# Splitting the running maximum in three bf16 parts, and the router's weights as one stationary matrix

## What is computed

```
log_D = where(tril, cs[:, :, None] - cs[:, None, :], -inf) + ig[:, None, :]
max_log_D = max(log_D, axis=-1)
D_mat = exp(log_D - max_log_D)
C = (q @ k.T) / sqrt(64) * D_mat
h = (C / (maximum(abs(C.sum(-1)), exp(-max_log_D)) + 1e-6)) @ v
x = x + tanh(g_xattn) * layernorm(h) * ln_scale

x2 = layernorm(x)
scores = softmax(x2 @ router_w.T)
topk_w, topk_idx = top_k(scores, 2)
x = x + tanh(g_ffn) * (routed experts(x2) + shared expert(x2))
```

## Time and profile before

| | us |
|---|---|
| median of 3 runs | 1300.96 (1299.69 to 1302.8) |
| the profiled execution | 1299.23 |
| its span in the trace | 1297.7 |

### The profile page before, as it was taken

One profiled execution on the slowest core, in us unless ns is written; L12 is line 12 of the kernel. 1 busy time (PEld: TensorE's weight loads), 2 busy tenths in 40 slices (PEclk: granted clock), 3 DMA queues, 4 the chain that ended last, 5 costly groups with the idle time before them and its releaser, 6 DMA issues.

```text
span 1297.7 us, 23994 instructions
## 1 busy us (share of the span) xinstructions
PE 1111.2 (86%) x6643; PEld 912.9 (70%) x6644; DVE 749.3 (58%) x1940; ACT 387.6 (30%) x852; POOL 478.2 (37%) x368
## 2 busy tenths in 40 slices
PE   3099999999999999999999876999999999999000
PEld 2066888888888888888888764788888888887000
DVE  2835667676677677676667634544444444444365
ACT  1132344443343344343343101233232322322000
POOL 3700021222213220322122335366656657700675
PEclk9565899999999999999999978999999999999555
DMA  6010010111001110111000244555564645331798
GB/s 206 17 48 33 1 64 4 66 65 65 32 32 65 65 59 6 65 48 49 12 23 34 82 168 143 192 173 183 162 194 162 203 153 178 129 113 65 217 301 265
DMA packets 57849, 134.37 MB, mean 104 GB/s; under 512 B 7088, under 2 KB 7088, under 8 KB 57808
## 3 DMA queue, kind: packets, MB, share of 16 engines
q0 software_dynamic: 17472, 59.78, 14.1%
q1 hardware_dynamic: 26128, 48.51, 11.4%
q10 hardware_dynamic: 14208, 25.57, 5.5%
HBM read 83.23 MB, written 50.59 MB: 103 GB/s over the span
## 4 chain that ended last, share of the span: by engine, by line
PE 84%; DVE 6%; DMA 6%; issue 2%; ACT 1%; POOL 1%; DVEq 0%; POOLq 0%; ACTq 0%
PE bank L1141 18%; PE bank L1006 15%; PE bank L1159 9%; PE bank L1017 7%; PE bank L953 6%; PE bank L921 5%; PE bank L944 4%; DMA area<-routed_y,y_at 4%; PE bank L887 4%; PE bank L955 3%; PE bank L1129 3%; PE bank L992 2%; PE bank L966 2%; PE bank L968 2%; PE bank L965 2%
## 5 line engine op out<-in xcount | busy, mean ns | idle before, releaser
L1141 PE MATMUL bank<-w_ring,x2nT 128*128 x960 | 243.7, 403 | 7.1 <-DVE x2nT L1624 7.0
L1006 PE MATMUL bank<-x2nT,w_ring 128*128 128x256 f32 x1536 | 206.3, 293 | 3.2 <-DVE sh_act L1426 3.2
L1141 PEld LDWEIGHTS bank<-w_ring,x2nT 128*128 128x128 f32 x960 | 175.7, 190 | 46.8 <-issue 11.8
L1006 PEld LDWEIGHTS bank<-x2nT,w_ring 128*128 128x128 f32 x1536 | 195.6, 199 | 3.8 <-issue 3.6
L492 POOL DMA_INDIRECT routed_x<-x2n,slot_u x64 | 63.2, 988 | 250.8 <-DVE slot_u L1418 236.2
L1159 PE MATMUL bank<-w_ring,sh_actT 128*128 x480 | 125.4, 396 | 2.3 <-DVE sh_actT L1619 2.3
L513 POOL TENSOR_TENSOR sh_actT<-sh_act,sh_actT 128x256 fp32r<-128x256 f32 x64 | 46.8, 732 | 203.8 <-ACT sh_actT L732 203.8
L609 POOL TENSOR_TENSOR w_ring<-area,one 128x3072 fp32r<-128x3072 f32 x14 | 74.2, 5303 | 114.5 <-PE bank L1159 114.5
L1606 DVE SCALAR_TENSOR_TENSOR ctxT<-ctxT,bank 128x256 f32<-128x256 f32 x80 | 33.7, 421 | 142.5 <-ACT ctxT L834 142.5
L1159 PEld LDWEIGHTS bank<-w_ring,sh_actT 128*128 128x128 f32 x480 | 90.0, 188 | 24.3 <-issue 3.0
L1017 PE MATMUL bank<-w_ring,sh_actT 128*128 128x512 f32 x384 | 102.4, 418 | 2.3 <-DVE sh_act L1426 1.4
(11 more groups left out here) (192 smaller groups left out, 2007.7 us busy)
## 6 DMA issues: line engine op xcount, KB each, us to landing
x2n<-routed_x SPq DMA_DIRECT2D x80, 256.0 KB, 2.7
routed_y<-cs_in ACTq DMA_DIRECT2D x80, 256.0 KB, 2.1
base_out<-in_x_dram SPq DMA_DIRECT2D x16, 512.0 KB, 4.8
cs_in<-in_ctx_dram SPq DMA_DIRECT2D x16, 512.0 KB, 3.5
area<-n_L_ffn_expert_gate_dram POOLq DMA_DIRECT2D x16, 512.0 KB, 4.1
area<-in_L_ffn_expert_up_dram POOLq DMA_DIRECT2D x16, 512.0 KB, 5.8
area<-n_L_ffn_expert_down_dram POOLq DMA_DIRECT2D x16, 512.0 KB, 7.1
out_dram<-area SPq DMA_DIRECT2D x32, 256.0 KB, 4.3
```

Of the source, the lines that this page charges most:

```text
L1006: last = mm(GU[m][:, at:at + S], w[:, w_part, c, m * P:(m + 1) * P], x2nT[:, x_part, c, :], start=(c + p == 0), stop=(c == DC - 1 and p == 2))
L1141: last = mm(bank[2 + t.par][:, :], xtT[:, x_part, t.par, c * P:(c + 1) * P], w_gu[:, bass.ds(slot, 1), w_part, c, :].rearrange("p a i -> p ...
```

## The change

The running maximum is kept in three bf16 parts instead of two fp32r ones, in rows 0, 32 and 64 on; `head_sel` is bf16 as well, and `spread` multiplies 96 rows, which makes its tile 128 x 128, like the mask product's. DVE has two more operations in `rows_end`, and `spread` waits for the eighth of them. The router has `router_wT`, padded with zeros to 128 columns, as stationary matrix and streams 256 tokens past it: 8 products. Their result has the tokens along the columns, so ACT copies 32 rows of it (`logit_row`), and PE turns them back with two float32 products against `pair_ident` (two stacked identities, which also add both parts; 32 rows, a tile of 32 x 128), in the new `logits_pe`, which stands ahead of `shared(G, 1)` on PE. DVE copies the logits from there. The start gets a memset of `router_wT` and the making of `pair_ident` on DVE, and a third selection for `head_sel` on POOL.

```diff
-        head_sel = sb("head_sel", [P, NH, P], F32R)
+        head_sel = sb("head_sel", [P, NH, P], BF16)
-        router_wT = sb("router_wT", [P, DC, 2 * E], F32R)
+        router_wT = sb("router_wT", [P, DC, P], F32R)
+        pair_ident = sb("pair_ident", [2 * E, E])
-        max_parts = sb("max_parts", [FG + NH, 2, S], F32R)
+        max_rest = sb("max_rest", [FG + NH, S])[FG:, :]
+        max_parts = sb("max_parts", [P, 2, S], BF16)
+        logit_row = sb("logit_row", [2 * E, S])
-        row_step = event("row_step", 6)
+        row_step = event("row_step", 8)
...
-                for part in range(2):
+                for part in range(3):
                     select(head_sel[:], 1.0, ALU.not_equal, -FG * part, 1, [[-1, NH], [0, P]])
...
+            def router(b):
+                act.wait_ge(router_made.sem, router_made.upto(b.n))
+                s.copy(logit_row[:, :], SM[0:2 * E, 0:S]).then_inc(logit_row_made.sem, 1)
...
                 if front:
                     max_hi(F)
                 if route:
+                    router(G)
                     shared(G, 0)
...
-                    mm(MB[k][:, at:at + n], head_sel[0:FG + NH, h, :], max_parts[:, b.par, S - n:S],
+                    mm(MB[k][:, at:at + n], head_sel[0:3 * FG, h, :], max_parts[0:3 * FG, b.par, S - n:S],
...
+                for c in range(DC):
+                    for part in range(2):
+                        last = mm(SM[:, 0:S], router_wT[:, c, :], x2nT[:, part, c, :],
+                                  start=(c + part == 0), stop=(c == DC - 1 and part == 1))
+                last.then_inc(router_made.sem, 1)
+
+            def logits_pe(b):
+                pe.wait_ge(wT_copied.sem, 9)
+                pe.wait_ge(logit_row_made.sem, logit_row_made.upto(b.n))
+                apart(pe)
                 for j in range(ST):
-                    for c in range(DC):
-                        for part in range(2):
-                            last = mm(SM[:, j * 2 * E:(j + 1) * 2 * E], x2nT[:, part, c, j * P:(j + 1) * P],
-                                      router_wT[:, c, :], start=(c + part == 0), stop=(c == DC - 1 and part == 1))
-                last.then_inc(router_made.sem, 1)
+                    last = mm(SM[:, j * E:(j + 1) * E], logit_row[:, j * P:(j + 1) * P], pair_ident[:, :],
+                              start=True, stop=True)
+                last.then_inc(logits_turned.sem, 1)
...
+                    logits_pe(G)
                     shared(G, 1)
...
                 shared_down(H, 1)
+                logits_pe(G)
                 rank(G, False, False)
...
+            v.memset(router_wT[:, :, :].bitcast(F32), 0.0).then_inc(wT_copied.sem, 1)
...
+            v.tensor_tensor(pair_ident[:, :], ident[0:2 * E, 0:E], ident[0:2 * E, E:2 * E], ALU.add
+                            ).then_inc(wT_copied.sem, 1)
...
-                v.tensor_tensor(max_parts[FG:, b.par, :], max_row[:, :], max_parts[0:NH, b.par, :], ALU.subtract
+                v.tensor_tensor(max_rest[:, :], max_row[:, :], max_parts[0:NH, b.par, :], ALU.subtract
                                 ).then_inc(row_step.sem, 1)
+                dve.wait_ge(row_step.sem, row_step.upto(b.n, 6))
+                v.tensor_copy(max_parts[FG:FG + NH, b.par, :], max_rest[:, :]).then_inc(row_step.sem, 1)
+                dve.wait_ge(row_step.sem, row_step.upto(b.n, 7))
+                v.tensor_tensor(max_parts[2 * FG:2 * FG + NH, b.par, :], max_rest[:, :],
+                                max_parts[FG:FG + NH, b.par, :], ALU.subtract).then_inc(row_step.sem, 1)
...
-                dve.wait_ge(router_made.sem, router_made.upto(b.n))
-                parts = SM[:, 0:ST * 2 * E].rearrange("p (j h n) -> p j n h", j=ST, h=2)
-                v.tensor_reduce(logits[:, :, :], parts, AX_X, ALU.add).then_inc(logits_made.sem, 1)
+                dve.wait_ge(logits_turned.sem, logits_turned.upto(b.n))
+                v.tensor_copy(logits[:, :, :], SM[:, 0:ST * E].rearrange("p (j n) -> p j n", j=ST)
+                              ).then_inc(logits_made.sem, 1)
```

More of the change, by code:

```diff
@@ L278, in flamingo_kernel @@
         router_made = event("router_made")
+        logit_row_made = event("logit_row_made")
+        logits_turned = event("logits_turned")
         logits_made = event("logits_made")
@@ L450, in other_constants @@
                 const(g.memset(mask_b[:], 0.0))
-                const(g.memset(head_sel[:].bitcast(F32), 0.0))
+                const(g.memset(head_sel[:], 0.0))
                 const(g.memset(v_aug[:], 1.0))
                 const(g.memset(taken[:], 0.0))
-                const(g.memset(max_parts[:].bitcast(F32), 0.0))
+                const(g.memset(max_parts[:], 0.0))
                 select(identb[:], 1.0, ALU.not_equal, 0, 1, [[-1, P]])
@@ L882, in _ @@
             last.then_inc(wT_made.sem, 1)
-            pe.wait_ge(wT_copied.sem, 6)
+            pe.wait_ge(wT_copied.sem, 7)
             def turn_tile(src):
@@ L1200, in _ @@
                               ).then_inc(wT_copied.sem, 1)
+            v.memset(router_wT[:, :, :].bitcast(F32), 0.0).then_inc(wT_copied.sem, 1)
+            dve.wait_ge(wT_copied.sem, 3)
             v.tensor_copy(router_wT[:, :, 0:E], pe_w[:, 3 * DC:4 * DC, :]).then_inc(wT_copied.sem, 1)
-            dve.wait_ge(wT_copied.sem, 3)
+            dve.wait_ge(wT_copied.sem, 4)
             v.tensor_tensor(router_wT[:, :, E:2 * E], pe_w[:, 3 * DC:4 * DC, :], router_wT[:, :, 0:E], ALU.subtract
@@ L1212, in _ @@
                             ).then_inc(wT_copied.sem, 1)
-            dve.wait_ge(wT_copied.sem, 7)
+            dve.wait_ge(wT_copied.sem, 8)
             dve.wait_ge(pool_const.sem, FIRST_CONSTS)
+            v.tensor_tensor(pair_ident[:, :], ident[0:2 * E, 0:E], ident[0:2 * E, E:2 * E], ALU.add
+                            ).then_inc(wT_copied.sem, 1)
             def base_tile(b, j):
@@ L1687 @@
 FIRST_CONSTS = 6
-POOL_CONSTS = 23
+POOL_CONSTS = 24
 TABLE_STEPS = 17
```

## The result

The changed kernel takes 1235.83 us (median of 4 runs, 1232.94 to 1243.62) against 1301.88 for the kernel before in the same comparison: a ratio of 0.9502, 95% interval 0.9454 to 0.9549. The forecast was 1231, the range 1221 to 1256.

The account below looks back on a forecast made before the run. TensorE was taken to bound the steady steps until DVE's chain is in the way. 1299.2 - 62 (14 steps) - 9 (first two steps) + 1 (start and end) = 1229, forecast as 1231 against the runs' median; range 1221 to 1256.

Parts of the forecast that it names:

- A head from 0.885 to 0.29 us: Spreads on TensorE: with all four products on 128 x 128, a head takes 0.29 us, a pair 0.58 instead of 1.68.
- The tile makes the gaps: Spreads on TensorE: leaving the tile costs about 0.1 us, changing the type nothing.
- The load of bf16 is hidden: Spreads on TensorE: bf16 weight loads overlap running products; a load costs at most 0.03 us.
- rival 3: Spreads: bf16 loads stand bare, 0.12 us a head, 0.96 a step, 13 in 14 steps: 1244 us; chance 0.05.
- 4.6 us a step, less 0.2 for waits: Steady steps: spreads save 4.5 us and the router 0.1, less 0.2 for waits that appear: minus 4.4 a step.
- DVE's 0.85 us more: Two new 8x256 operations on DVE ahead of the shared expert's product add 0.85 us, hidden, but barely.
- The router, minus 0.82 and plus 0.66: Router in each step: eight wide products save 0.82 us, turning products cost 0.66 to 0.80; together minus 0.1.
- +0.5 on the turning products: In the drain, the turning products stand ahead of the last rank: plus 0.5 us.
- The first steps, minus 9, and one more step: First two steps, 62 to 130 us, mostly at the lower clock: 2 x 4.9 = 9.8 us less, taken as 9.
- minus 4.4 us a step, times 14: The 14 steady steps from 130 to 721 us: 4.4 us less each, minus 62 in all.
- rival 1: DVE's chain takes over the steps, 38.5 instead of 37.1 us each: 50 us less, 1251; chance 0.17.
- rival 4: TensorE's short waits cost it the full clock in the loop, a step 19 us longer: 1326 us; chance 0.03.

Follow-up runs that it names:

- e11: The changed kernel with 114 semaphore increments that nobody waits for at the head of DVE's program: 1209.36 us, ratio 0.9283.
- e1: The kernel before with spreads multiplying 96 rows instead of 40, both operands still fp32r: 1238.14 us, ratio 0.9526.
- e2: The kernel before with head_sel and max_parts in bf16, still two parts and 40 rows: 1268.15 us, ratio 0.975.
- e5: The changed kernel with 140 semaphore increments at the head of DVE's program: 1231.09 us, ratio 0.9478.
- e12: The changed kernel's spreads alone, router as in the kernel before, with 118 increments at the head of DVE's program: 1215.21 us, ratio 0.9349.
- e9: The kernel before with 128 semaphore increments at the head of DVE's program: 1300.66 us, ratio 0.9998.
- e10: The changed kernel with 118 semaphore increments at the head of DVE's program: 1210.91 us, ratio 0.9292.
- e8: The kernel before with 150 semaphore increments at the head of DVE's program: 1309.55 us, ratio 1.0072.
- e4: The changed kernel with 112 semaphore increments at the head of DVE's program: 1238.42 us, ratio 0.9519.
- e3: The kernel before with 16 semaphore increments that nobody waits for at the head of DVE's program: 1308.98 us, ratio 1.0065.

## Why the forecast was right, and where it was not

The time was forecast within 0.4%, but by errors that cancel, and that is luck. With the loop's code in a good place the same work takes 1209 us (`e11`): 92 us less than before where the sum had 70, and below the stated range of 1221 to 1256. The waits at the returns, which the prediction didn't have, took 26 of them back. By stages, in the two profiled executions (measured, and what the sum had):

| stage | measured | the sum |
|---|---|---|
| to the first gate products (28.49 to 29.53) | +1.0 | +0.5 |
| gates of sequences 1 to 4: 138.9 to 119.7 | -19.2 | -13 |
| twelve steps: 503.3 to 472.3 | -31.0 | -53 |
| the last step, drain, tables: 131.2 to 123.9 | -7.3 | -4 |
| experts and gathering | +0.8 | 0 |

- *A head from 0.885 to 0.29 us*: 0.29 measured. *The tile makes the gaps*: shown by `e1` and `e2`, each alone. *The load of bf16 is hidden* (against rival 3): a bf16 load lasts 0.10 us in the trace of the changed kernel, and slots of 0.11 and 0.06 leave no room for it bare. The Trainium skill's stricter rule on overlap ("TensorE: Matmul & The Clock Gate", Part 3) doesn't hold for these loads.
- *4.6 us a step, less 0.2 for waits*: 4.57 measured in an undisturbed step, and no such waits in it. DVE's 0.85 us more are hidden as computed, with 0.32 us to spare.
- *The router, minus 0.82 and plus 0.66*: 0.75 less and 0.64 more, as said. In the drain the sign was wrong: I put +0.5 on the turning products and had no term for the clock under the narrow ones, which gave 3.3 back.
- *The first steps, minus 9, and one more step*: 19.2 measured against 13. A pair at the lower clock behaved as priced (1.04 us where 1280 columns make 1.07). The 6 us beyond the sum fit the clock: 0.68 over the 138.9 us of this stage before and 0.71 over the 119.7 after, so some 44 us lost to it before and 34 after. How long it stays low differs from run to run: `e5`, with the same work as the changed kernel, takes 110.8 us for the stage.
- *The loop in the kernel before* had three steps of 43.1 us among those of 41.5, with 5 us at a clock of 0.66 in one of them, ahead of which TensorE had not waited. In `e1`, `e2`, `e11` and `e12` the steps are all alike. That is 4.7 us I had not counted on either. What makes these dips I don't know.
- *The step that failed* is "minus 4.4 us a step, times 14", with 0.2 us a step put on waits that appear: measured are 4.57 us a step and, at four returns, 7 us each the other way. It took all that DVE does to be its operations. The two operations and the new constants are also instructions: the loop's body grew from 376 to 379 of them and its place moved by 10 (the traces' records of DVE count the same), and with that code that had stayed resident was fetched anew at each return. Of the 59.5 us that twelve steps gain in `e11`, 28.6 were lost. Of rival 1 (DVE's chain takes over) the sign appeared, TensorE waiting for DVE on head 0's output, exactly at the place that I had named as the tightest; but its cause was another, and the chain itself holds nothing back: in `e11` TensorE never waits in the twelve steps. Of rival 4 (the clock falls in the loop) the sign appeared too, behind each of these waits, for 3 to 7 us and not for good.

The reading of the pieces: of ten different places of DVE's loop, counted in instructions ahead of it, those that begin at 320, 444, 446 and 448 have no waits and those at 330, 336, 442, 464, 470 and 476 do (320 and 336 are the kernel before, without and with 16 increments, 448 both `e9` and `e10`). The one picture I know that fits all is four pieces of 128 kept, of which one is always the next ahead, so that a loop of 376 or 379 stays only where it lies in three. Then 444 is at the very front of a piece, and 320 four or five behind it: the kernel before had its place by luck, with a handful of instructions to spare. That it is kept in four pieces is inferred from these places and from five fetches a turn, not seen. The Trainium skill ("Runtime: NRT & Kernel Launch", Instruction fetch mechanics) says that a taken branch to code outside the kept window forces a fetch before execution goes on, and that such an engine holds 512 instructions. The waits and packets at the returns agree with the first, and four pieces of 128 come to the same 512, by inference; the 256 instructions that the page gives as a block don't fit `e5` and `e8` beside the other places.

## What to carry to other kernels

Products that alternate between tiles of the array pay about 0.1 us at each change, whatever their types; padding the smaller one with rows of zeros took 0.44 us off a head in `e1`, and the rows themselves show no price (0.36 us for a product of 96 rows, 0.38 for the one of 40). Before a forecast, read the place and length of each engine's loops as well as its operations: where the page shows more packets of instructions than before, or an engine stands at the head of a loop with "issue" as releaser, shift the loop by instructions in an idle stretch and measure again. A slack that covers a fault in the slow kernel is gone in the fast one: the same fault cost 2 us a return before and 7 after. And a time that comes out as forecast is no proof of the sum: compare it stage by stage.

## What the runs showed of the hardware

- A change of the array's tile costs 0.1 us (0.16 against 0.06 us for 128 bf16 columns, `e2`); a head with four changes takes 0.68 us in bf16 and 0.29 with none. What alternating types and fp32r loads cost together on one tile is 0.15 us a head (`e1`, 0.44).
- DVE's code comes in packets of 8192 bytes. A loop of 379 instructions in a bad place leaves DVE standing for 3.6 to 6.0 us at each return (the changed kernel, `e4`, `e5`), and in a good place it doesn't (`e10`, `e11`). 16 increments ahead of it decided that in `e3`; 128 changed nothing in `e9`.
- Behind a wait of 4.5 us TensorE's granted clock was 0.54 for the next 6.7 us; it had been 1.0 before. Behind a wait of 0.87 us it was 0.54 for 6.6 us (`e3`).
- In the drain, sixteen products of 32 columns ran at a clock of 0.69 to 0.76 in seven kernels and at 1.00 in one (`e1`); eight of 256 columns ran at 1.0 in all six that have them.
